# A gated cross-attention and mixture-of-experts block: tokens scattered to expert slots in DRAM by indirect DMA, loops written out, one program block

## What is computed

```
x = x + tanh(g_x) * (softmax(q k^T / 8) v @ Wo + bo)      # q from layernorm(x), k and v from ctx
xf = layernorm(x).reshape(4096, 256)
logits = xf @ gate_w.T;  scores = softmax(logits);  topv, topi = top_k(scores, 2)
gates = topv / sum(topv);  cap = 1024
loc = running count of tokens of this expert, all first choices first, then all second choices
flat_idx = where(loc < cap, topi * cap + loc, 0)
disp[flat_idx] += xf                                       # expert e gets rows e*1024 ...
eo = relu(disp_e @ fc1_e.T + b1_e) @ fc2_e.T + b2_e
x = x + tanh(g_f) * sum over the two choices of eo[flat_idx] * gates * (loc < cap)
```

## Time and profile before

| | |
|---|---|
| median of 3 runs | 1038.72 us (1037.49 to 1039.75) |
| profiled execution, its own time | 1034.84 us |
| its span, first to last instruction | 1033.1 us, mean granted TensorE clock 0.991 |
| busy: TensorE, DVE, ACT, GpSimd | 988.0, 684.1, 478.7, 481.0 us |
| instructions | 21103 |
| DMA | 63.42 MB, 61 GB/s over the span |

### The profile page before, as it was taken

One profiled execution on the slowest core, in us unless ns is written; L12 is line 12 of the kernel. 1 busy time (PEld: TensorE's weight loads), 2 busy tenths in 40 slices (PEclk: granted clock), 3 DMA queues, 4 the chain that ended last, 5 costly groups with the idle time before them and its releaser, 6 DMA issues. The chain is left out here.

```text
span 1033.1 us, 21103 instructions
## 1 busy us (share of the span) xinstructions
PE 988.0 (96%) x7314; PEld 850.9 (82%) x7314; DVE 684.1 (66%) x1607; ACT 478.7 (46%) x1502; POOL 481.0 (47%) x498
## 2 busy tenths in 40 slices
PE   6899999999999999999999997899999999999995
PEld 5678878778878878878878786799999999999995
DVE  6886895886886886886885866444455554445552
ACT  3663553553553653553553630434353544535351
POOL 7521071081180270270360244385757658585756
PEclk9999999999999999999999998999999999999998
DMA  8201110110010021011001001324436162423525
GB/s 250 83 19 44 42 59 5 39 61 20 20 61 33 7 61 41 0 61 61 0 1 62 2 1 45 130 53 116 78 98 146 44 142 41 127 56 103 126 53 66
DMA packets 49949, 63.42 MB, mean 61 GB/s; under 512 B 5977, under 2 KB 41715, under 8 KB 49907
## 3 DMA queue, kind: packets, MB, share of 16 engines
q1 hardware_dynamic: 37234, 45.41, 13.6%
q0 software_dynamic: 12672, 17.47, 10.0%
HBM read 46.45 MB, written 16.78 MB: 61 GB/s over the span
## 5 line engine op out<-in xcount | busy, mean ns | idle before, releaser
L1260 ACT ACTIVATE hid<-up,b 128x512 f32<-128x512 f32 x128 | 88.3, 690 | 84.0 <-PE up L1211 84.0
L729 ACT ACTIVATE work<-score,negmax 128x128 f32<-128x128 f32 x256 | 90.4, 379 | 79.0 <-DVE negmax L926 79.0
L729 ACT ACTIVATE probs_odd<-score,negmax 128x128 f32<-128x128 f32 x256 | 90.4, 381 | 52.1 <-DVE negmax L926 52.1
L1139 POOL DMA_INDIRECT out_dram<-eo,index_e x64 | 104.6, 1634 | 19.5 <-issue 19.2
L1312 DVE TENSOR_TENSOR eo_raw<-down,b 128x256 f32<-128x256 f32 x64 | 25.9, 425 | 124.0 <-PE down L1225 124.0
L350 POOL TENSOR_SCALAR var<-mv 128x4 f32<-128x4 f32 (+1 forms) x17 | 3.9, 227 | 216.7 <-DVE mv L781 210.5
L1305 DVE TENSOR_TENSOR hid_l<-hid,hid_h 128x512 fp32r<-128x512 f32 x128 | 88.6, 692 | 4.4
L682 ACT ACTIVATE q_sb<-proj 128x512 f32<-128x512 f32 x64 | 38.7, 604 | 104.4 <-PE proj L600 104.4
L1268 ACT ACTIVATE eo<-eo_raw,gate_e 128x256 f32<-128x256 f32 x64 | 30.9, 507 | 120.9 <-DVE eo_raw L1312 120.9
L1303 DVE CAST hid_h<-hid 128x512 fp32r<-128x512 f32 x128 | 55.1, 430 | 45.8 <-ACT hid L1260 44.0
L926 DVE TENSOR_REDUCE negmax<-score 128x4 f32<-128x512 f32 x128 | 81.8, 680 | 0.8 <-PE score L521 0.8
(11 more groups left out here) (217 smaller groups left out, 3061.8 us busy)
## 6 DMA issues: line engine op xcount, KB each, us to landing
w_raw<-fc1T_dram SPq DMA_DIRECT2D x9, 1024.0 KB, 5.4
w_raw<-fc_dram SPq DMA_DIRECT2D x9, 1024.0 KB, 9.8
rows<-x_dram SPq DMA_DIRECT2D x16, 512.0 KB, 4.1
out_dram<-rows SPq DMA_DIRECT2D x8, 512.0 KB, 2.8
xn_rows<-rows SPq DMA_DIRECT2D x8, 512.0 KB, 2.8
c_raw<-ctxT_dram SPq DMA_DIRECT2D x8, 256.0 KB, 3.7
c_raw<-ctxT_dram SPq DMA_DIRECT2D x16, 128.0 KB, 4.4
b<-fc2b_dram SPq DMA_DIRECT2D x9, 128.0 KB, 9.0
```

What stands on the lines that cost most here:

```text
L729: last = nc.scalar.activation(probs[j % 2][:, c, :], score[hh][:, b * P:(b + 1) * P], ACT.Exp, bias=negmax[:, j % 2, c:c + 1], accum_out=s ...
L1139: pool.indirect_dma_start(out=out_rows[:, :], out_offset=bass.IndirectOffsetOnAxis(ap=index_e[par][:, half * GB + i:half * GB + i + 1], ax ...
L1260: nc.scalar.activation(hid[m % 2][:, :], up[m % 2][:, :], ACT.Relu, bias=b1[par][:, m:m + 1]).then_inc(s_hid, 1)
```

## The change

- Instead of the table, each group's rows are scattered at once. `packed` holds for every token its normalised row, its number and `exp(top2 - top1)` (258 words). Once its slots are known, GpSimd writes it with 8 indirect DMAs (2 choices x 4 batches of 128 rows) to `disp`, a DRAM array of 8192 slots. Slots of unused places are beyond the bound and written by nobody. SP fills `disp` beforehand with blank rows (zeros, token number 4096).
- So the one-hots, T0/T1, the table, `xn2_rows` and the gathers go. The rows come back by plain loads on SP, 516 KB for a group; DVE's `meta` takes slot numbers and gates from the last two columns, at the start of each group.
- `dispatched` waits at the end of GpSimd's iteration until the scatters have landed (in iteration 0 until the blank rows have); DVE waits for it before it writes the next `xn2` (j=2) and `slots` (j=5), SP before the first load of the experts.
- In `finish` the low parts of expert 0's weights move from GpSimd to DVE: w1 before the residual, w2 after routing; ACT's high part of w2 moves behind the last exponential. The extra matmuls of 3 and 6 go, 24 become 40; the 26 at the start of the experts go too.
- All hardware loops are written out, and attention and experts share one program block.
- In SBUF, `fixed`, `packed` and `first` come, `table`, `tanh_g`, `zrow` and one quarter of `rows` (4096 bytes a partition, ahead of `aT_h`) go; in the experts `eo` takes the place of `rows`.

The diff, cut to its core (renamed semaphores and the removed one-hots left out):

```diff
@@ jobs
-MISC_PREV = {1: ["O0", "O1"], 2: ["XA", "XB"], 3: ["LG"], 4: ["PR"], 7: ["T0", "T1"]}
+MISC_PREV = {1: ["O0", "O1"], 2: ["XA", "XB"], 3: ["LG"], 4: ["PR"]}
@@ SP, attention
-            sp.wait_ge(s_xn2_ready, whole)
-            sp.dma_start(xn2_v[:, bass.ds(g * GB, GB), :], xn2).then_inc(s_xn2_out, 16)
         iteration(0, 1, False)
+        sp.wait_ge(s_blank, 1)
+        sp.dma_start(disp.rearrange("(t p) w -> p t w", p=P),
+                     blank[:, :].unsqueeze(1).to_broadcast([P, E * CAP // P, W])).then_inc(s_blank_out, 16)
...
-        sp.wait_ge(s_xn2_out, 16 * NG)
+        sp.wait_ge(s_disp_done, NG + 1)
@@ GpSimd, attention
+        def dispatch(g):
+            pool.wait_ge(s_disp_done, g)
...
+            me.mark(nc.gpsimd.tensor_scalar(token[:, :], token[:, :], float(TOK), None, ALU.add))
+            me.after()
...
+            copy(packed[:, :, D], token[:, :]).then_inc(s_packed, 1)
+            pool.wait_ge(s_gexp, g)
+            pool.wait_ge(s_slot_ready, g)
+            pool.wait_ge(s_packed, g)
...
+            for j in range(2):
+                for b in range(GB):
+                    pool.indirect_dma_start(
+                        out=disp[:, :], out_offset=bass.IndirectOffsetOnAxis(ap=slots[:, j, b:b + 1], axis=0),
+                        in_=packed[:, b, :], in_offset=None,
+                        bounds_check=E * CAP - 1, oob_is_err=False).then_inc(s_disp, 16)
+        def dispatched(g):
+            if isinstance(g, int) and g == 0:
+                pool.wait_ge(s_blank_out, 16)
+            else:
+                pool.wait_ge(s_disp, 16 * 2 * GB * g)
+            pool.sem_inc(s_disp_done, 1)
...
             if has_prev:
-                onehots(nc.gpsimd, 0).then_inc(s_onehot0, 1)
...
+                dispatch(g)
             if has_next:
...
                 copy_ck()
+            dispatched(g)
@@ GpSimd, finish
-            pool.wait_ge(s_e0_hi, 1)
-            nc.gpsimd.tensor_tensor(wq_l[:, :, :], w1_raw[:, :, :], wq_h[:, :, :].bitcast(f32), ALU.subtract)...
...
-            pool.wait_ge(s_e0_hi, 2)
-            nc.gpsimd.tensor_tensor(wo_l[:, :, :], w2_raw[:, :, :], wo_h[:, :, :].bitcast(f32), ALU.subtract)...
...
+            dispatch(NG)
+            dispatched(NG)
@@ TensorE, finish
-                wait_warm(3)
-                wait_warm(6)
-            wait_warm(24)
-            for half in range(2):
-                misc(f"T{half}", proj[half], NG)
+            wait_warm(40)
@@ DVE, finish
+            dve.wait_ge(s_e0_hi, 1)
+            low(wq_l[:, :, :], w1_raw[:, :, :], wq_h[:, :, :]).then_inc(s_e0_lo, 1)
             residual_start(NG)
...
+            route_slots(NG)
+            V.tensor_tensor(first[:, :, :], rank[:, :, :], ..., ALU.is_lt).then_inc(s_first_done, 1)
+            dve.wait_ge(s_e0_hi, 2)
+            low(wo_l[:, :, :], w2_raw[:, :, :], wo_h[:, :, :]).then_inc(s_e0_lo, 1)
@@ experts
-                gather(index_e[1 - par], half)
-                scatter(n, e, par, half)
+                scatter(2 * e + half, e, par, half)
+        def load_rows(e, half):      # SP; after meta of the same half
+            src = disp_v[bass.ds(e, 1), half * TOK:(half + 1) * TOK, :]
+            sp.dma_start(rows[half][:, :, :], src.rearrange("o (i p) w -> p (o i) w", p=P)).then_inc(rows_in[half], 16)
-        wait_warm(26)
-        transpose_rows(16 * GB, 0)
+        transpose_rows(16, 0)
         wait_warm(6)
+        def meta(n, e, half):        # DVE
+            dve.wait_ge(rows_in[half], 16 * (e + 1))
+            if not (isinstance(e, int) and e == 0):
+                dve.wait_ge(scatters[half], 16 * GB * e)
+                dve.wait_ge(s_eo_ready, GB * n - GB)
+            weight = rows[half][:, :, D + 1]
+            V.tensor_copy(index[half][:, :], rows[half][:, :, D])
+            i = me.mark(V.tensor_scalar(den[:, :], weight, 1.0, None, ALU.add))
+            i = me.mark(V.tensor_tensor(share[:, :], weight, first[...], ALU.max))
+            i = me.mark(V.reciprocal(den[:, :], den[:, :]))
+            V.scalar_tensor_tensor(out=gate[half][:, :], in0=share[:, :], scalar=tanh_g[:, 1:2], in1=den[:, :],
+                                   op0=ALU.mult, op1=ALU.mult).then_inc(s_meta, 1)
...
-        with pe.Fori(1, TURNS) as t:
+        for t in range(1, TURNS):
```

More of the change, by code:

```diff
@@ L23 @@
 HK = H // P
-NHI = E * CAP // P
 EH = CAP // P
-PAD = 1
+W = D + 2
 BIG = 65536.0
@@ L152, in attention @@
     xn2T = work[:, 1024:2048].rearrange("p (k t) -> p k t", k=DK)
-    onehot_lo = work[:, 1024:2048].rearrange("p (s k) -> p s k", s=8)
-    rows = sb("rows", [P, 4, GB, D])
-    xn, xr, x1, xn2 = (rows[:, n] for n in range(4))
+    rows = sb("rows", [P, 3, GB, D])
+    xn, xr, x1 = (rows[:, n] for n in range(3))
     flat_rows = rows.rearrange("p a b d -> p a (b d)")
-    wv_raw, wk_raw = [work[:, 0:INNER], flat_rows[:, 1]], [flat_rows[:, 2], flat_rows[:, 3]]
-    hi_vals = rows[:, 3].rearrange("p b (two c) -> p (b two) c", two=2)
     q_sb, k_sb = sb("q_sb", [P, TOK]), sb("k_sb", [P, TOK])
@@ L300, in _ @@
         iteration(1, 2, True)
-        with sp.Fori(2, NG - 1) as g:
+        for g in range(2, NG - 1):
             iteration(g, g + 1, True)
@@ L450, in _ @@
         start = me.n
-        per = 4
-        with pool.Fori(1, NG - 1) as g:
+        per = 5
+        for g in range(1, NG - 1):
             me.enter((g - 1) * per + start)
@@ L1093, in step @@
         def step(e, nxt, par, first=False):
-            if not first:
+            if first:
+                sp.wait_ge(s_e0_lo, 2)
+            else:
                 sp.wait_ge(s_w_lo, e)
-            for half in range(2):
-                sp.wait_ge(gathers[half], 16 * GB * (e + 1))
             load_expert(sp, fc1T, fc2, nxt, w1_raw, w2_raw, s_w_in)
@@ L1106, in _ @@
         step(1, 2, 1)
-        with sp.Fori(1, TURNS - 1) as t:
+        for t in range(1, TURNS - 1):
             for i in range(EB):
@@ L1119, in _ @@
     def _(pool):
-        def columns(e, par):
-            nc.gpsimd.tensor_copy(index_e[par][:, :], index[:, bass.ds(e * EH, EH)]).then_inc(s_index_e, 1)
-        def gather(columns_, half):
-            pass_gate(pool, s_pool_gate)
-            for i in range(GB):
-                pool.indirect_dma_start(
-                    out=rows[half][:, i, :], out_offset=None, in_=xn2_dram[:, :],
-                    in_offset=bass.IndirectOffsetOnAxis(ap=columns_[:, half * GB + i:half * GB + i + 1], axis=0),
-                    bounds_check=N + PAD - 1, oob_is_err=False).then_inc(gathers[half], 16)
         def scatter(n, e, par, half):
@@ L1152, in split_low @@
                                     ALU.subtract).then_inc(s_w_lo, 1)
-        nc.gpsimd.memset(index[:, NHI:NCOL], N).then_inc(s_index_pad, 1)
-        pool.wait_ge(s_index, 1)
-        gather(index, 0)
-        gather(index, 1)
-        pool.wait_ge(s_index_pad, 1)
-        columns(0, 0)
         def step(e, par):
             split_low(e + 1, 1 - par)
-            if not (isinstance(e, int) and e == 0):
-                for done in scatters:
-                    pool.wait_ge(done, 16 * GB * e)
-                pass_gate(pool, s_pool_gate)
-            columns(e + 1, 1 - par)
-            pool.wait_ge(s_index_e, e + 2)
             for half in range(2):
-                n = 2 * e + half
-                pool.wait_ge(s_rt_ready, 2 * n + 2)
-                gather(index_e[1 - par], half)
-                scatter(n, e, par, half)
+                scatter(2 * e + half, e, par, half)
         step(0, 0)
         step(1, 1)
-        with pool.Fori(1, TURNS) as t:
+        for t in range(1, TURNS):
             for i in range(EB):
                 step(EB * t + i, i)
-        for half in range(2):
-            pool.wait_ge(gathers[half], 16 * GB * (E + 1))
         for done in scatters:
@@ L1188, in _, with transpose_rows @@
         mm = nc.tensor.matmul
-        def transpose_rows(gathered, half):
-            pe.wait_ge(gathers[half], gathered)
+        def transpose_rows(loads, half):
+            pe.wait_ge(rows_in[half], loads)
             for k in range(DK):
@@ L1273, in _ @@
             group(n, n // 2, n // 2, n % 2)
-        with act.Fori(1, TURNS) as t:
+        for t in range(1, TURNS):
             for i in range(2 * EB):
@@ L1299, in group @@
                 dve.wait_ge(biases[par], 16 * (e - par) + 32)
-                V.tensor_copy(gate_e[par][:, :], gate[:, bass.ds(e * EH, EH)])
+            meta(n, e, half)
             for m in range(HK):
@@ L1318, in _ @@
             group(n, n // 2, n // 2, n % 2)
-        with dve.Fori(1, TURNS) as t:
+        for t in range(1, TURNS):
             for i in range(2 * EB):
```

255 lines of the change are left out of this document (96 added, 159 removed).

## The result

The changed kernel took 1062.91 us in the median of four runs (1061.70 to 1065.63); the kernel before took 1038.11 beside it (1037.18 to 1039.75). The ratio is 1.024, 95% interval 1.0224 to 1.0256: slower, where 1021.8 was forecast. On three other chips, though, the changed kernel, in this text or with its loops put back, ran 1.7 to 2% faster than the kernel before. Which chip a kernel runs on turned out to be a part of the answer, and the experiments need it: a letter stands for each, A for that of the result.

What follows compares the result with a forecast made beforehand. TensorE, busy 96% of the span, was taken as the bound, other engines mattering only where it waits. The terms -15.1 - 1.3 + 1.5 - 0.3 - 1.7 = -16.9 gave 1021.8 us from a median of 1038.72; range 1013 to 1032.

Steps and rivals of the forecast that it cites:

- Parts 1 and 3: Attention loop: table matmuls T0 and T1 go from six turns, -15.1 us; scatters replace GpSimd's one-hots, +1.5.
- the allowance of 1.5: Attention loop: GpSimd's eight scatters 0.9 us longer beside DVE, so K stalls 0.25 us in six turns.
- rivals (a) and (c): Scatters as costly as accumulating ones, 1049.8 us, chance 0.12; T0 and T1 covered another wait, 1029.3, chance 0.14.
- The 72.8 us named as the sign: Attention loop: iterations 72.8 us apart and not 75.35 would show the forecast right.
- Part 2: Iteration 7: DVE's one-hots no longer hold back its row maxima, -1.3 us.
- Part 4: Hand-over from routing to experts: slots earlier, rows landing 2.8 us earlier, clock loss +2.5; -0.3 us in all.
- The clock: Hand-over: TensorE idles until the rows land, its clock falls to half rate; +2.5 us, between 0 and +4.
- Part 5: Experts: SP loads rows, DVE makes index and gate in idle time, TensorE sees none of it; 0 us.
- the +-3.3: Experts: the down matmuls' two rates might become all fast or all slow, +-3.3 us, at 0 in the sum.
- Part 6: End of the kernel: without gathers on GpSimd the last scatter starts earlier, -1.7 us.
- Part 3: Attention loop: eight scatters replace 21 one-hot operations on GpSimd before K's copies; +1.5 us, from 0 to 24.
- (a): Loop and hand-over: plain scatters cost as much as accumulating ones, 1.93 us start to start; +11.1, 1049.8 us, chance 0.12.

Runs made afterwards that it cites:

- again: The changed kernel, nothing edited, run again on another chip: 1014.34 us, 0.9801 of the kernel before.
- again2: The changed kernel, nothing edited, run once more on a further chip: 1016.69 us, 0.9832 of the kernel before.
- paced: The changed kernel with a 0.61 us copy ahead of each loop scatter and K's copies between the two fours: 1023.28 us, 0.9859 of the kernel before.

## Why the prediction was wrong, step by step

The mechanism was right and one cost was missing. Undisturbed (`again`: span 1012.4, own time 1014.14, against 1033.1 and 1034.84 before) the sum is -20.7 where -16.9 was forecast, and 1014 lies in the range, 1013 to 1032:

- Parts 1 and 3. The six turns take 72.62 us in the mean, not 75.35: -16.3, for -15.1 + 1.5. The scatters start 1.28 apart (1.30 said), the first takes 1.10, the copies for K end at 223.65 and hold nobody (K starts at 224.54): the allowance of 1.5 was too careful, and rivals (a) and (c) didn't come about. The 72.8 us named as the sign is 72.6, and 72.8 in `again2`; the last microsecond of this term lies between runs.
- Part 2: iteration 7's turn is 62.26 for 63.30: -1.04, for -1.3.
- Part 4: from the last projection to the first down matmul 58.21 for 59.80: -1.6, for -0.3. The slots come 24.95 us after the projection's start, for 30.5 before: -5.6, of -6.1. The rows land at +42.6, for +45.2: -2.7, of -2.8. In these rows is an error that the total hid: the split of w2 that moves to DVE holds the first scatter for 1.35 us. The clock fell as said, but was back at 2.4 GHz at 635.96, before the first up matmul (636.38), so it costs 1.3 in place of 2.5.
- Part 5: 354.4 for 355.1 us from the first down matmul to the last: -0.7, for 0; within the +-3.3 that stood beside it. The two rates of down matmuls stayed as they were, eight groups at 118.7 ns and eight at 114.4 in both kernels, one after the other in `again`.
- Part 6: from the last down matmul to the end -1.9, for -1.7. But the sign named for it failed: the last scatter starts 1.4 us after its input (1005.11 against 1003.72), not within 0.8, since the accumulating scatters stand 1.86 apart.
- Start: the first projection is 0.8 later, for 0, and 0.1 later in `again2`; unrolling is not shown to be the cause.

The step that failed is Part 3, and what it left out is not a term of GpSimd's time, which it had right: it is TensorE's wait for updates, which it put at nothing by leaving them out: on some chips, while a row of eight indirect DMAs 1.28 us apart is issued, TensorE's semaphore updates are held back. Against the undisturbed span the profile after has 40.4 us more in the six turns, 6.4 in the next and 0.9 at the hand-over, of 47.5 in all. No rival had this: (a) came nearest to the time (1049.8) by another way, a slow scatter at 1.93 us, which did not occur.

Could the profile of before have warned? It has such a row of gathers 1.30 apart at the start of the experts, but no matmul that anybody waits for there, and in the experts they mix with accumulating scatters, which stand over 1.8 apart. The attention part, where the new DMAs go, had none. If that profile stems from a chip without the stall, it could not have shown it anywhere. A resource that the trace of before does not show in that place deserved a bound upwards; mine came only from issue times.

What stays open: what in the chip couples GpSimd's indirect DMAs to TensorE's updates and not to those of DVE or ACT; why chips differ (A, D and E show it, B, C and F do not), or whether it is the hour; and why the first scatters of iteration 1 pass without it (there the first late update falls behind the sixth, in iteration 2 one is 0.26 late behind the second and the next 5.82 behind the third).

## What to carry to other kernels

Indirect DMAs in a row have a rate as well as an issue time: where a row of them lies beside matmuls that somebody waits for, leave about 1.9 us from start to start (the least pause that was tried and sufficed here), and read TensorE's waiters for "remote". When a kernel's time disagrees with a sum that its stages bear out, run the unedited kernel on another chip before explaining: here four edits "cured" what one unedited run also lacked. Whatever is put in order to space DMAs has a price by its neighbours: copies beside DVE's normalisation lengthen it, waits for landing cost 0.8 us of waking each.

## What the runs showed of the hardware that was not expected

- TensorE's semaphore updates can reach their waiters up to 8.6 us after the matmul, and then several within 0.2 us (in iteration 1 of the profile after at 151.16, 151.22, 151.28 and 151.34); no other engine's did.
- Chips that show it also run the kernel before some 2 to 3 us slower (1037.5 to 1038.1, against 1034.8 to 1035.7).
- Traces from chips D and E and the profile after lack the times of 59 to 71 semaphore updates, even `paced`, in which none came late; those of B, C, F and G lack 0 to 3. So the missing times mark such a chip where no update is late.
- An indirect DMA of 32 rows takes GpSimd 0.87 to 1.02 us, one of 128 rows 0.97, and one whose rows all lie beyond the bound 0.97 to 1.12: nearly all of it is fixed. Eight plain DMAs of 128 rows take 4.43 in all.
